# A third narrow chunk's resident columns ahead of the streamed tiles, in a bank freed by moving the projections of product four

## What is computed

```python
z = leaky_relu(lap_mul(A, x) @ W1 + b1)            # product 3
d2 = sq[:, None] + sq[None, :] - 2.0 * (z @ z.T)
S = exp(-sqrt(max(d2, 0) + 1e-10) / 2)             # keep the 4 largest of each row
A2 = S_top4 + A                                     # a search over 4096 columns per row
out = lap_mul(A2, x) @ W2 + b2                      # product 4: dense A part, and 4 rows gathered and mixed
x = layernorm(x + out)
x = layernorm(x + maximum(concat([x, A @ x]) @ W.T + b, 0))   # product 5
```

## Time and profile before

| what | us |
|---|---|
| median of 3 runs (1463.95, 1469.2, 1472.29) | 1469.2 |
| the profiled execution's own time | 1465.6 |
| its span, first to last instruction | 1463.7 |
| PE busy | 1393.7 (95%) |
| DVE busy | 836.0 (57%) |
| ACT busy | 451.0 (31%) |
| POOL busy | 246.9 (17%) |
| matmuls of the profiled execution | 7300 |

### The profile page before, as it was taken

The page is one execution under the profiler, slowest core; times in us unless marked ns, Lnnn a source line. Parts: engine busy times, 40 slices in busy tenths (PEclk is TensorE's granted clock), DMA queues, the critical chain, the costliest instruction groups (busy, mean ns, idle before and its releaser), DMA issues.

```text
span 1463.7 us, 20350 instructions
## 1 busy us (share of the span) xinstructions
PE 1393.7 (95%) x7300; PEld 737.9 (50%) x7300; DVE 836.0 (57%) x1311; ACT 451.0 (31%) x979; POOL 246.9 (17%) x358
## 2 busy tenths in 40 slices
PE   6999999999999799999999987999999889999997
PEld 4776676666444354444544532444444344444454
DVE  6877766665224423323322269999999356555044
ACT  4776665665100000000000045666666200000011
POOL 2111110111100100000000000111111277774000
PEclk9999999999999999999999999999999989999999
DMA  9999998897998979788778520004443799999962
GB/s 311 400 383 389 365 331 300 325 318 266 359 382 331 379 308 346 306 316 328 298 292 310 227 72 1 15 17 137 134 130 115 242 370 401 380 386 394 352 234 71
DMA packets 112814, 403.26 MB, mean 276 GB/s; under 512 B 10368, under 2 KB 28384, under 8 KB 91232
## 3 DMA queue, kind: packets, MB, share of 16 engines
q1 hardware_dynamic: 72672, 314.33, 57.8%
q0 software_dynamic: 20576, 77.07, 14.0%
q10 hardware_dynamic: 19488, 10.80, 2.4%
HBM read 337.67 MB, written 64.49 MB: 275 GB/s over the span
## 4 chain that ended last, share of the span: by engine, by line
PE 70%; DVE 10%; DMA 10%; issue 7%; ACT 2%; POOL 0%; ACTq 0%; SPq 0%; DVEq 0%; POOLq 0%
PE acc L1137 10%; PE acc L1138 9%; PE acc L1139 9%; PE pt L1201 4%; DMA at_scratch<-region 3%; PE pt L1277 3%; PE pt L1278 3%; PE pt L1279 3%; DVE hT L1021 3%; PE pt L1137 3%; PE pt L1139 3%; PE pt L1138 3%; DMA region<-in_adj 3%; PE acc L1186 2%; PE acc L1182 2%
## 5 line engine op out<-in xcount | busy, mean ns | idle before, releaser
L1137 PE MATMUL acc<-region,yop 128*128 128x512 f16 x681 | 259.6, 381 | 16.6 <-DMA region<-at_scratch 16.6
L1201 PE MATMUL pt<-ident,region 128*128 128x128 f32 x1024 | 243.1, 277 | 18.8 <-DMA region<-in_adj 9.6
L1138 PE MATMUL acc<-region,yop 128*128 128x512 f16 x681 | 259.5, 381 | 0.0
L1139 PE MATMUL acc<-region,yop 128*128 128x512 f16 x681 | 259.5, 381 | 0.0
L969 DVE SCALAR_TENSOR_TENSOR region<-pt,region 128x512 f16<-128x512 f32 x200 | 135.3, 686 | 76.9 <-ACT region L631 76.4
L1201 PEld LDWEIGHTS pt<-ident,region 128*128 128x128 f32 x1024 | 145.9, 143 | 61.2 <-issue 16.1
L677 ACT ACTIVATE region<-pt 128x512 f32<-128x512 f32 x256 | 132.8, 602 | 109.4 <-PE pt L1284 95.8
L631 ACT ACTIVATE region<-pt 128x512 f16<-128x512 f32 x200 | 117.8, 596 | 108.6 <-PE pt L1201 94.0
L1021 DVE MAX8 hT<-region 128x8 f32<-128x4096 f32 x32 | 141.2, 4411 | 2.4 <-ACT region L677 2.4
L1137 PEld LDWEIGHTS acc<-region,yop 128*128 128x128 f16 x681 | 66.7, 98 | 98.7 <-issue 14.6
L598 ACT ACTIVATE std<-mv,eps_ln 128x4 f32<-128x4 f32 x32 | 9.5, 297 | 334.5 <-DVE mv L803 334.5
(11 more groups left out here) (235 smaller groups left out, 2157.8 us busy)
## 6 DMA issues: line engine op xcount, KB each, us to landing
region<-at_scratch SPq DMA_DIRECT2D x166, 1280.0 KB, 7.8
region<-in_adj SPq DMA_DIRECT2D x64, 1024.0 KB, 8.9
at_scratch<-region POOLq DMA_DIRECT2D x40, 768.0 KB, 7.0
at_scratch<-region POOLq DMA_DIRECT2D x40, 512.0 KB, 7.6
region<-at_scratch SPq DMA_DIRECT2D x76, 256.0 KB, 2.7
x_scratch<-xout ACTq DMA_DIRECT2D x16, 256.0 KB, 12.3
gath_all<-x_scratch POOLq DMA_DIRECT2D x12, 256.0 KB, 4.1
xin<-at_scratch SPq DMA_DIRECT2D x12, 256.0 KB, 2.8
```

The costliest lines, as they stand in the source:

```text
L1137: nc.tensor.matmul(into, y[:, 0, kt, :], high, start=(kt == first_tile), stop=False)
L1138: nc.tensor.matmul(into, y[:, 0, kt, :], low, start=False, stop=False)
L1139: return nc.tensor.matmul(into, y[:, 1, kt, :], high, start=False, stop=(kt == last_tile))
L1201: ins = nc.tensor.transpose(pt[kt % 4][:, t * P:(t + 1) * P], nat[u % 4][:, t, (kt % TPC) * P:(kt % TPC + 1) * P], ident[:, :])
```

## The change

A third chunk, 6, has its kept columns done early, in `pt[2]`; chunk 7 goes into `pt[0]`. Product 4's projections move from `pt[2]` to `pt[3]`, behind the last use of `pt[3]` for x2, while product 5's stay in `pt[2]`. The waits follow: product 4's first projection waits for the last `yw`, the first turn of product 5 waits until DVE has read product 4's last projection, and `bank_left` gives chunk 7 of product 4 as the holder of `pt[0]` and chunk 5 as that of `pt[1]` (before: 6 and 7). Projections of x2 and the turn stay where they were. No matmul, load or copy is added or removed.

```diff
-NARROW_KEPT = [4, 5]
+NARROW_KEPT = [4, 5, 6]
+NARROW_BANK = {4: 0, 5: 1, 6: 2, 7: 0}
@@
-        late_nat = pt[2][:, :].rearrange("p (t f) -> p t f", t=TPC)
+        late_nats = {p: pt[b][:, :].rearrange("p (t f) -> p t f", t=TPC) for p, b in ((4, 3), (5, 2))}
@@
-                return wide[c] if c < WIDE else pt[c % 2][:, :]
+                return wide[c] if c < WIDE else pt[NARROW_BANK[c]][:, :]
@@
             elif p == 5:
                 pe.wait_ge(xT_ready, nth(XTS, 4, NCH - 1))
-                pe.wait_ge(yw_ready, NCH)
+                pe.wait_ge(nat_read, nth(ALL, 4, NCH - 1))
@@
+            if p == 4 and c == 0:
+                pe.wait_ge(yw_ready, NCH)
             if not (p == 0 and first(c)):
                 pe.wait_ge(nat_read, n - 1)
-            into = late_nat if p >= 4 else pnat[:, :, :]
+            into = late_nats[p] if p >= 4 else pnat[:, :, :]
@@
                 if c == NARROW_KEPT[0]:
                     pe_project_x2(pe, NCH - 2)
-                else:
+                elif c == NARROW_KEPT[1]:
                     pe_turn(pe, 4, NCH - 1)
@@
             def bank_left(c):
                 if c < len(wide5):
-                    return nth(ALL, 4, c if c < WIDE else c + NCH - len(wide5))
+                    return nth(ALL, 4, c if c < WIDE else max(b for b in NARROW_BANK if NARROW_BANK[b] == c - WIDE))
                 return nth(ALL, 5, c - len(wide5))
```

More of the change, by code:

```diff
@@ L825, in residual @@
                     held = res_rows(half, c, 1)[:, 0, within, :]
-                    last = nc.vector.scalar_tensor_tensor(held, late_nat[:, t, :],
+                    last = nc.vector.scalar_tensor_tensor(held, late_nats[4][:, t, :],
                                                           dinv2[:, c * TPC + t:c * TPC + t + 1], held, ALU.mult, ALU.add)
@@ L874, in epilogue @@
                 if p == 5:
-                    nc.vector.tensor_tensor(t_nat[:, :, :], late_nat, over_tiles(bias[5]), ALU.add).then_inc(nat_read, 1)
+                    nc.vector.tensor_tensor(t_nat[:, :, :], late_nats[5], over_tiles(bias[5]), ALU.add).then_inc(nat_read, 1)
                     dve.wait_ge(nat_read, n)
```

## The result

| | before | changed |
|---|---|---|
| median, 20 runs each (us) | 1469.55 | 1472.95 |
| lowest to highest (us) | 1463.95 to 1474.23 | 1469.39 to 1478.29 |
| profiled execution, its own time (us) | 1465.6 | 1471.36 |
| its span (us) | 1463.7 | 1469.4 |

What follows compares the result with a forecast made beforehand. The prediction took the DMA engines as the scarce thing from about 1150 to 1365 us. Terms +4.5, -0.2, -4.5 and zeros sum to -0.2, about +0.1 us with small upward bounds: 1469.3 us, range 1463.5 to 1475.

Steps and rivals of the forecast that it cites:

- +4.5 us ahead of the wide rest, shifting the whole tile stage: 21 matmuls inserted on PE before the wide rest: +4.5 us, with tile loads and PE's waits for them shifting equally.
- rival A: At the wide rest: the tile burst doesn't shift, the matmuls fit inside PE's waits, 4.7 us gained, 1464.6; chance 0.14.
- -0.2 us for ACT's copy of x2: PE's small wait at 1151.37 for ACT's copy of the turned x2 goes: -0.2 us.
- The residual loads entering sooner, 0 between -0.6 and +1.0: In the wide rest, POOL's loads enter 1.5 us sooner relative to PE's tiles: 0, bounds -0.6 and +1.0 us.
- The lead of 1.7 us at chunk 6's last unit: At chunk 6, the unit loads' lead over PE falls from 6.2 to 1.7 us and holds: no new wait, 0.
- Rival B: Unit loads fall behind at chunk 6, PE waits there and in product 5: +2.5 to +6.5 us; chance 0.18.
- The banks, 0: Product 5's column in `pt0` waits for ACT's copy of chunk 7, which ends 0.6 us in time: 0.
- Rival C: ACT's copy for `pt0` is late, mixing having slipped 4.5 us or more: +0.9 us, no more than 2; chance 0.10.

Runs made afterwards that it cites:

- e5: The rotated banks of e2, with chunk 6's kept columns moved inside the wide rest, behind kt 29: ratio 0.9964 to the kernel before, median 1463.56 us.
- e9: The changed kernel with two output buffers for mixing instead of one: ratio 1.0002 to the kernel before.
- e1: The changed kernel with the kept columns of chunks 4 and 5 only done early, so new banks and waits with the old order: ratio 0.9991 to the kernel before.
- e2: The changed kernel with pt banks rotated, so that no column of product 5 lies in chunk 7's bank: ratio 0.9996 to the kernel before.
- e8: Rotated banks of e2, kept columns and wide tiles in turn, plus the early residual loads of e6: ratio 0.9922 to the kernel before, median 1457.86 us.
- e12: e11 with two output buffers for mixing: ratio 0.9916 to the kernel before, median 1457.60 us.
- e6: The kernel before, with three of POOL's four residual x2 loads issued ahead of the last group's work: ratio 0.9965, median 1463.43 us.
- e11: e8 with the projection of group 6's x2 moved between kt 24 and 25: ratio 0.9916 to the kernel before, median 1455.57 us.
- e3: The changed kernel with ACT's copy of chunk 7's sum ahead of the end of mixing of chunk 3: ratio 0.9996 to the kernel before.
- e4: The changed kernel with the last projection of x2 one tile of the wide rest earlier: ratio 1.0025 to the kernel before.

## Why the prediction was right and where it failed

- *+4.5 us ahead of the wide rest, shifting the whole tile stage*: right. The trace shows 4.5 us, and e5 shows the reverse side, since the same work gained some 4.6 us by the medians once it stood where PE waited. Of rival A at most the 0.6 us are left by which the tile waits shrank (12.7 to 12.1).
- *-0.2 us for ACT's copy of x2*: the line is gone from the waits.
- *The residual loads entering sooner, 0 between -0.6 and +1.0*: product 5 began 0.8 us sooner behind the turn than before. Of that 0.2 is the line above; the other 0.6 are the tile waits, at the lower bound, on one pair of traces. So the term from the shares of the queues, and with it what the Trainium skill's "DMA: Bandwidth & Descriptors", section "Queues, rings and completion order", would have added by taking turns, did not show as a loss.
- *The lead of 1.7 us at chunk 6's last unit*: right almost to the digit. The unit issued at 1229.3 landed 12.0 us later, at 1241.3; PE's first matmul of it starts at 1242.9, five tiles ahead of chunk 6's end at 1246.2: 1.6 us. Rival B had no part in the result.
- *The banks, 0*: **wrong, and this is the step that failed.** The working said that mixing follows the gathers, so the copy ends 3.0 us later than before, at 1269.0 on the old trace's scale. It ended at 1273.67 - 1.63 = 1272.0. The store ahead of it (L603 at 1265.00, L604 at 1272.60 now) went out 6.0 us later behind the turn, not 3.0. Of these 6.0 us, 3.6 are the gathers' later start and 0.5 had been added by chunk 0's layernorm. The last 1.9 came between the layernorms of chunks 0 and 3, where DVE waited 4.4 us for stores instead of 2.1. The working took that store as an instruction on ACT to be passed and not as a transfer whose landing the next chunk needs; it put these waits at nothing without a reason. e9 agrees: with a second buffer chunk 3's layernorm came 2.0 us sooner than in the changed kernel. The 2.4 us of e1 warn that a part of such a difference may be scatter. PE in turn came 0.8 us sooner. So 0.6 us of slack became 3.0 + 0.8 - 0.6 = 3.2 us of wait. Rival C named the place and the wait, but capped it at 2 us; it cost 5.0, with 1.7 us of clock in it.
- The two halves of the change meet in that store. Kept columns use no unit, so no slot comes free while PE works on them, and SP's queue pauses. In the trace before no unit was issued between 1223.9 and 1231.7 us (chunk 6) and between 1245.6 and 1253.3 us (chunk 7). The stores of chunks 1 and 2, issued at 1225.6 and 1244.3, each met one of these pauses and took 14.5 and 11.4 us. After the change only the second pause is left (1246.4 to 1254.1), and they took 18.8 and 20.3 us. I had counted the pause as lead for the units alone. The other traces agree. In all ten that show these landings and have chunk 6's kept columns moved (the changed kernel, e2 to e5, e8 to e12), the two stores took 18.4 to 20.6 us; in e6, where they stay, 14.9 and 14.2. No run varied the pause by itself.
- The chances: faster 0.04, same 0.89, slower 0.07 at the 0.5% bound; the result is on the slow side within it. That it lies inside the range is partly luck: the range reached to 1475 for rival B, which had no part, while C with its cap of 2 us would have ended at 1471.3.

## What to carry to other kernels

Work moved ahead of a stage that waits for transfers gains nothing if those transfers are started by the stage's own progress: it has to stand among the waits (e5), or other transfers have to leave that stage (e6), or both (e11). Where a step needs a buffer again, price the landing of the store that holds it, from the stretches in which the DMA engines are full, and check it against what else the same edit takes away from those engines. And where an in-order engine copies a sum out for one consumer behind work for another, either its order (e3) or the bank (e2) unties the two for nothing.

## What the runs showed of the hardware

A store of 256 KB on ACT's queue took 20.3 us beside full unit loads. The next one took 7.8 us. PE's wait had lengthened a pause of the SP queue: no unit was issued between 1268.0 and 1280.1 us, 12.2 us, where e2 without the wait has 7.1 us. In e2 and e3, where PE didn't wait, that store took 18.5 and 18.2 us. The queues from 1251 to 1271 us in the changed kernel (packets, MB, share of 16 engines):

```profile
q1 hardware_dynamic: 749, 6.83, 84.1%
q0 software_dynamic: 506, 1.03, 13.6%
q10 hardware_dynamic: 528, 0.26, 4.5%
```

The store is 528 packets of 0.5 KB beside 749 packets of 9.1 KB; it got as many turns as its neighbours within a factor of 1.5, and 4.5% of the time. This agrees with the Trainium skill's "DMA: Bandwidth & Descriptors", section "Queues, rings and completion order", by which each engine takes its queues in turn, packet by packet. It does so as far as the packets that the profile counts, here one for each row of a transfer, are the packets of that rule; no run here shows that.

PE's granted clock fell to its lower level behind waits of 3.18 us (changed kernel) and 3.39 us (e4) in an otherwise unbroken stream. The same work that followed took 1.7 and 2.9 us more than before. Behind a wait of 1.26 us (e9) the clock stayed at 1.00 and nothing was added. Of waits in between no run tells. In this kernel a wait of over 3 us has to be priced at one and a half times to twice itself.
